# VectorE's step reordered: a pair's low part first, then the sum of the pair after it

## The reference, cut to what matters

```python
x = x + _L0_cond_ref(x, itok_B_0_7, L0_cond_weights, fside_8xS_0)   # out = einsum('bct,bcd->bdt', x, w[subject]) + b[subject]
x = x + _L1_cond_ref(x, W, A, Bm, scalings, itok_B_0_6)             # out = x W^T + scalings[k] * (x A[k]^T) Bm[k]^T, k per batch
```

## Time and profile before

| | |
|---|---|
| median of 3 runs | 254.08 us |
| profiled execution, its time | 255.75 us |
| its span, first to last instruction | 254.0 us |
| granted TensorE clock, mean | 0.996 |
| busy: TensorE, VectorE, ScalarE, GpSimd | 238.5, 138.9, 111.4, 79.6 us |

### The profile page before, as it was taken

How to read it: one execution, slowest core, us unless ns; L and a number is a source line. 1 busy time by engine, 2 the same in 40 slices (tenths; PEclk the granted TensorE clock), 3 DMA queues, 4 the chain that set the end, 5 groups by cost and what they waited for, 6 DMA issues and landing times.

```text
span 254.0 us, 9847 instructions
## 1 busy us (share of the span) xinstructions
PE 238.5 (94%) x2932; PEld 196.1 (77%) x2933; DVE 138.9 (55%) x241; ACT 111.4 (44%) x189; POOL 79.6 (31%) x283
## 2 busy tenths in 40 slices
PE   1888998999999999999999999999999999999993
PEld 1767885888878887888878887878878888888882
DVE  5277567666475656565574757474774745243300
ACT  2262544443643536353634435353535434342511
POOL 4367520355006510454015700466342413000000
PEclk9999999999999999999999999999999999999998
DMA  6745364464646564555646463655547364641331
GB/s 174 177 148 166 107 185 101 120 181 127 206 102 196 131 180 134 141 156 152 191 103 199 131 194 95 171 143 162 165 124 207 101 198 119 201 123 54 85 83 41
DMA packets 24147, 36.68 MB, mean 144 GB/s; under 512 B 6594, under 2 KB 6594, under 8 KB 24130
## 3 DMA queue, kind: packets, MB, share of 16 engines
q1 hardware_dynamic: 17536, 27.28, 39.2%
q10 hardware_dynamic: 6594, 9.18, 12.6%
HBM read 19.66 MB, written 16.78 MB: 143 GB/s over the span
## 4 chain that ended last, share of the span: by engine, by line
PE 85%; issue 3%; DVE 2%; POOL 1%; POOLq 1%; ACT 1%; ACTq 1%; DVEq 0%
PE ps L782 70%; PE ps L761 13%; PE ps L737 2%; PE ps L701 1%; POOLq L227 1%; POOL bias_pair L377 1%; POOL p_pair L366 1%; DVE m_f L486 1%; ACT x_hi L598 1%; DVE m_lo L492 0%; ACTq L624 0%; DVE x_lo L518 0%; DVE a_parts L473 0%; ACT m_hi L592 0%; DVE b_parts L479 0%
## 5 line engine op out<-in xcount | busy, mean ns | idle before, releaser
L782 PE MATMUL ps<-m_hi,x_hi 128*128 x264 | 105.8, 401 | 0.0
L782 PE MATMUL ps<-m_hi,x_lo 128*128 x264 | 103.3, 391 | 0.0
L782 PE MATMUL ps<-m_lo,x_hi 128*128 x264 | 103.3, 391 | 0.0
L518 DVE TENSOR_TENSOR x_lo<-x,x_hi 128x512 fp32r<-128x512 f32 x64 | 44.7, 698 | 80.4 <-ACT x_hi L598 80.3
L366 POOL COPY p_pair<-p_all 64x64 f32 x128 | 42.3, 331 | 126.0 <-issue 77.3
L598 ACT ACTIVATE x_hi<-x 128x512 fp32r<-128x512 f32 x64 | 40.4, 632 | 46.7 <-DVE x L510 28.2
L607 ACT ACTIVATE o_ring<-ps 128x512 f32<-128x512 f32 x60 | 35.7, 596 | 57.1 <-PE ps L782 56.9
L782 PEld LDWEIGHTS ps<-m_hi,x_hi 128*128 128x128 f32 x264 | 49.8, 189 | 11.1 <-issue 0.2
L782 PEld LDWEIGHTS ps<-m_hi,x_lo 128*128 128x128 f32 x264 | 49.8, 189 | 10.7
L782 PEld LDWEIGHTS ps<-m_lo,x_hi 128*128 128x128 f32 x264 | 49.9, 189 | 9.8
L510 DVE TENSOR_TENSOR x<-ps,bias_pair 128x512 f32<-128x512 f32 x64 | 43.6, 682 | 5.6 <-PE ps L761 5.6
(11 more groups left out here) (90 smaller groups left out, 62.3 us busy)
## 6 DMA issues: line engine op xcount, KB each, us to landing
x_ring<-in_x_dram SPq DMA_DIRECT2D x128, 128.0 KB, 2.7
out_dram<-o_ring SPq DMA_DIRECT2D x64, 128.0 KB, 2.3
out_dram<-o_ring ACTq DMA_DIRECT2D x64, 128.0 KB, 2.4
a_f<-in_L_cond_A_dram SPq DMA_DIRECT2D x8, 128.0 KB
o_ring<-in_L_cond_W_dram SPq DMA_DIRECT2D x2, 256.0 KB, 4.6
o_ring<-in_L_cond_W_dram ACTq DMA_DIRECT2D x2, 256.0 KB, 5.6
b_nat<-in_L_cond_Bm_dram ACTq DMA_DIRECT2D x1, 256.0 KB, 3.5
p_all<-in_L_cond_weights_dram SPq DMA_DIRECT2D x2, 128.0 KB, 6.7
```

The costliest lines, as they stand in the source:

```text
L518: nc.vector.tensor_tensor(x1_lo[:, u % HELD], x1[:, u % 2], x1_hi[:, u % HELD], ALU.subtract).then_inc(x1_lo_ready, 1)
L782: mm = nc.tensor.matmul(ps[:, bank, :], part[:, u % HELD, c, :], m[:, ds(k * (TC * T) + c * T, T)], start=(c == 0 and part is x1_hi and m ...
```

## The change: which operation stands first in VectorE's step

Step j of VectorE held A(j+2) and then S(j+2). It now holds S(j+2) and then A(j+3). Where the sum's first-layer result comes from the quad that TensorE does in the next step (u mod 4 = 1), the sum stands at the end of the step, behind `m_add`; in the other steps it stands ahead of `m_split`, of `a_split` and `b_split`, and of `m_add`. No operation is added or removed, no other engine's program is changed, and no wait's value is changed.

```diff
                 if not isinstance(j, int) or 2 <= j < PAIRS - 2:
-                    x1_add(j + 2, u + 2)
                     x1_split(j + 2, u + 2)
+                adds = not isinstance(j, int) or 1 <= j < PAIRS - 3
+                if adds and u % L0_QUAD != 1:
+                    x1_add(j + 3, u + 3)
                 for place_at, chunk in split_at(j, u, n):
                     m_split(place_at * TC + chunk, chunk)
                 if n is not None and u == HEAD:
                     a_split(n + 2)
                     b_split(n + 2)
                 for place_at, chunk in tiles_of(j, u, n):
                     m_add(place_at * TC + chunk, chunk)
+                if adds and u % L0_QUAD == 1:
+                    x1_add(j + 3, u + 3)
```

## The result

The changed kernel takes 259.61 us (median of 4 runs, 259.12 to 262.44); the kernel before takes 254.34 us (median of 4). The ratio is 1.0227, with a 95% interval from 1.0187 to 1.0266, so the change makes the kernel slower by 5.3 us. The longest of the four runs, 262.44 us, had the lowest granted TensorE clock, a mean of 0.974 against 0.993 to 0.999 in the others. The forecast was 257.4 us with a range of 255.4 to 258.8: right in sign and place, too small, and the measured time lies outside the range.

The account below looks back on a forecast made before the run. TensorE was taken to bound the kernel, with nearly all other engines' work hidden except at a few waits. Later quads at u = 6 gave 0.70 + 5 × 0.52 = 3.3 us, added to the median: 257.4 us, range 255.4 to 258.8.

Parts of the forecast that it names:

- what bounds the kernel, and where the change acts: TensorE is busy 238.5 of 254.0 us; the change counts at its few waits, six of them ahead of quads at u = 6.
- The quad's wait for A(7): At u = 6: removing this wait alone is worth 0.42 us in each of five passes and 0.90 in pass 0.
- the delay of `b_split`: On VectorE: 0.42 us from A(6) putting off `m_add`, plus 0.61 from A(7) as one more operation behind S(6).
- The product's delay against its turn: Product ahead of the quad at u = 6, pass 2: starts at 100.85, 0.56 us late, waiting for `b_split`.
- So the quad starts 0.8 us after `b_split`'s end.: TensorE at u = 6: register work queued behind the product's wait sets this lag, 0.28 us to L227 plus 0.53 to the quad.
- My upper bound for the lag: From `b_split`'s end to the quad: at most some 0.9 us (0.10, 0.71 and a register instruction), at least 0.42.
- forecast 0.70: Pass 0: the quad at u = 6 starts at 45.45 instead of 44.75, 0.70 us later.
- forecast 5 × 0.52: Passes 1 to 5: each quad at u = 6 starts 0.52 us later, as in pass 2 (101.55 instead of 101.03).
- The faster rival: Both sums fill only VectorE's idle time ahead of S(6), `b_split` keeps its time; 3.0 us gained, 251.1 us; chance 0.05.
- The limit it gave, 0.57 us: The `b_split` delay that decides the faster case: 100.32 + 0.71 against `b_split`'s end plus 0.80.
- The second rival: The sequencer runs ahead of the waiting product, the quad follows it by 0.32 us; 1.0 us lost, 255.1 us; chance 0.06.
- The third rival: `m_add`'s delay is hidden, A(7)'s is not; each quad 0.1 us later, 0.6 us lost, 254.7 us; chance 0.07.

Follow-up runs that it names:

- e1: Changed kernel with sums in steps that have an `m_add` back behind it (A(6), A(10)), A(7) still ahead of `m_split`; 256.65 us, ratio 1.0094 to the kernel before.
- e2: Changed kernel with A(7) back behind `b_split` in the loop's step u = 4, A(6) still ahead of `m_add`; 257.50 us, ratio 1.0100 to the kernel before.
- e3: Changed kernel with A(6) back behind `m_add` and A(7) back behind `b_split`, other sums still a step early; 254.64 us, ratio 0.9996 to the kernel before.
- e6: Changed kernel with the quad's waits and table-entry reading put ahead of the product in TensorE's program; 256.53 us, ratio 1.0086 to the kernel before.
- e4: Changed kernel, but A(6) and A(7) both behind `m_add` in step u = 3, A(10) and A(12) behind `m_add` too; 252.78 us, ratio 0.9947 to the kernel before.
- e5: e4 with `a_split` and `b_split` also put ahead of `m_split` in step u = 4; 251.59 us, ratio 0.9900 to the kernel before.
- e7: e5 with TensorE's waits and table-entry reading also put ahead of the product; 251.33 us, ratio 0.9884 to the kernel before.
- e0: The kernel before, without any edit, run once more for a second profile; 256.19 us in one run.

## Why the prediction was wrong in size

**Right: what bounds the kernel, and where the change acts.** The six quads at u = 6 were the place. The quad's wait for A(7) went, the product's wait came, and e1, e2 and e3, with the rows on A(10), show that A(6) and A(7) are the two causes and the only ones.

**Right: the delay of `b_split`.** Forecast 0.42 + 0.61 = 1.03 us behind S(5); measured 6.98 − 5.96 = 1.02. The product's delay against its turn was forecast at 0.56 us and is 0.55 (0.78 − 0.23) in pass 2.

**The step that failed first: "So the quad starts 0.8 us after `b_split`'s end."** It is 0.99 us. I had put together the register instructions L748, L749 and L227 from their rows, and left out that the quad has a third wait with an instruction of its own, the one for x1: the row at L754 in the changed kernel, L750 before. (So in the kernel before it is L750, at 100.4, and not L227, at which the quad waits for A(7).) It takes 0.1 us in the row of starts (101.2, 101.3, 101.4). The other 0.09 us are rounding in the reading: these rows give starts to 0.1 us only. By the trace itself 0.12 us pass from `b_split`'s end to the first instruction in both kernels (0.08 taken), and 0.57 from L227's first row to the quad (0.53 taken). That is 0.19 us in each of six passes, 1.1 us. My upper bound for the lag, 0.9 us, lay too low as well.

**The second: TensorE's wait for the last tile was not in the sum.** I asked for each moved operation who waits for it in the loop, where the split of the fourth tile is far ahead of its use. In step 53, where a quad no longer stands between, the reserve was under 0.3 us, and A(54) ahead of `m_add` took it: 0.38 us are lost. The rows of e1 and e3, where that sum is behind `m_add`, have 13.39 us in this stretch; after, e2 and e6, where it is ahead, have 13.77 to 13.80.

**The sum as measured.** From the loop to the end the changed kernel takes 226.09 − 221.05 = 5.04 us more: 1.03 in pass 0 (forecast 0.70), 5 × 0.71 in the others (forecast 5 × 0.52), 0.38 at the last tile (forecast nothing), and under 0.1 spread elsewhere. With the two corrections the forecast would have been 3.3 + 1.1 + 0.4 = 4.8 us. Of the rest, some 0.15 us in pass 0 belong to the profiled execution and not to the change: S(5), which stands ahead of the moved sums, already started 8.18 us behind the quad of step 2, where it is 8.02 in the kernel before and also in e6, whose VectorE program is that of the changed kernel. The spans of the two profiles differ by only 3.5 us, since the quad of step 2 started 1.54 us earlier in the execution of after that was profiled, by the scatter of the start (last section). That the spans meet the forecast of 257.3 so closely is chance.

**The rivals.** The faster rival fell as the prediction said, by a delay of 1.02 us. The limit it gave, 0.57 us, is wrong: its own numbers make it 101.03 − 100.52 = 0.51, and with the measured lag of 0.99 it is 0.32. The rival's idea holds where both sums stand in the idle time behind `m_add`: of its 3.0 us e4 gained 1.6, and e5, which also has `b_split` ahead of `m_split`, 2.7. The second rival, a sequencer that runs ahead of the waiting product, fell too. The wait for `b_split` is a sequencer instruction of 4.58 us; e6 moved the work ahead of it and got 0.49 us a pass back. The Trainium skill (Perfetto Trace Analysis, Tensor Engine Instruction) has it that a matmul waits in a queue while the sequencer goes on to the next instruction. That rule doesn't reach this wait: the matmul ahead of which it stands has three waits, and the trace shows two of them in an instruction by itself, at which the sequencer stood still for the 4.58 us. The third rival fell with ScalarE's `m_round`, whose wait for `m_add` went from 0.38 to 0.78 us.

## What to carry to other kernels

An operation that is pulled ahead of a chain is free if the engine would have idled there, or if nobody waits closely for what it puts off (A(10)): VectorE idled 1.26 us ahead of S(6), and the same two sums placed in that gap, behind `m_add`, made the kernel 0.5% faster, while a little further up and down they made it 2.3% slower. In front of a wait, list all that the waiting engine's sequencer has queued behind it, every wait and register read included. That work starts only when the wait passes, even while the engine still has matmuls to run (in e4 the quad came 1.04 us behind `b_split` although the product was on time), and moving it ahead of the wait gives it back. And follow each delayed result to its last use, outside the loop too.

## What was not expected of the hardware

The loop repeats to 0.1 us from one execution to another, and the scatter of this kernel's times lies mostly in the start: over ten profiles of these kernels the quad of step 2 started between 26.45 and 29.70 us, with no relation to the edits. It goes with the granted TensorE clock. Between 22 and 26 us this was full in after, e1, e4, e5 and e6, whose quads start at 26.45 to 27.02 us. Its mean was 0.72 in e7, 0.69 in e0, 0.60 in e2 and 0.50 in e3, whose quads start at 28.33, 28.89, 28.73 and 29.70. The rows of after and e3 for these 4 us (the third number from the end is the clock, the first after the length TensorE's busy time):

```profile
22.00:26.00 4.00, 4.00 (x21) 3.31 (x20) 1.66 (x3) 1.60 (x3) 3.00 (x12) 1.00 0.61 170
22.00:26.00 4.00, 4.00 (x11) 3.13 (x10) 1.32 (x2) 0.46 (x1) 2.74 (x10) 0.50 0.57 174
```

TensorE was busy throughout in both, but did 21 matmuls at 2.4 GHz and 11 at 1.2. The second layer's twelve matmuls of step 0 take 2.87 us in after (0.23 apart) and 5.26 in e3 (0.43 apart), which is 2.39 of the 2.89 us between their quads. In the first profile of the kernel before, the record of the clock only begins at 23.1 us; its matmuls stand 0.43 us apart up to there and 0.23 behind it. Why the clock rises at another time in another execution stays open.

The reading of a table entry into a register also varies: the rows shown here have 0.30 us, but it took 0.37 in pass 0 of e7 and 0.56 to 0.65 at the quads of all six passes of e5. What sets it stays open.
